# Values of two head groups in one projection, tokens stationary, and reordered query projections, in a one-core vision-tower kernel

## The chip, the core and the metric

The kernel runs on one core of a Trainium2 chip. The metric is the device time of one execution in microseconds, median of several. TensorE (PE) multiplies, VectorE (DVE), ScalarE (ACT) and GpSimd (POOL) do the element-wise work, and SyncE (SP) issues the DMAs.

## The reference

Three layers are computed one after the other for 8 batches of 256 tokens by 512 features:

```python
h = _L0_tok_ref(x, ...)                    # a long complex exponential sum: the mixer, (8, 256, 512)
h = h + attn(layernorm(h), w_q, w_k, w_v, w_o)
h = h + ffn(layernorm(h), ...)             # gated selection among 8 low-rank updates

# attn: 16 query heads, 4 key/value heads, head size 128
q = (x @ w_q).reshape(b, s, 16, 128).transpose(0, 2, 1, 3)
k = (x @ w_k).reshape(b, s, 4, 128).transpose(0, 2, 1, 3)
v = (x @ w_v).reshape(b, s, 4, 128).transpose(0, 2, 1, 3)
q, k = q * cos + rotate_half(q) * sin, k * cos + rotate_half(k) * sin
k, v = repeat(k, 4, axis=1), repeat(v, 4, axis=1)
scores = einsum('bhqd,bhkd->bhqk', q, k) / sqrt(128)
probs = softmax(scores + bias)             # causal
out = einsum('bhqk,bhkd->bhqd', probs, v)
out = out.transpose(0, 2, 1, 3).reshape(b, s, 2048) @ w_o
```

## The kernel before

**Stages.** The mixer comes first (to about 99 us of the profile), with tables built by DVE, ACT and POOL, and small matmuls in `chunk` (L1420). Its result goes through device memory (`mixed`) into the tile `x`, which holds all 8 batches. Attention follows. Its unit is a step: one batch `b` for one head group `g`, where a group is one key/value head with its four query heads. There are 4 groups of 8 batches, so 32 steps, `i = b + 8 * g`. The last layer's work is threaded into the steps of group 3 (`needs_ffn`, `needs_finish`, `needs_norm2`), and the first norm and the transposes of its tokens into those of group 0 (`needs_norm1`, `needs_xt`). Such threaded pieces are called hooks here.

**Order.** It is written out by hand: every engine has its own program, with a function `step(g, b, at)` in each, and semaphores between them. `RUNS` (L94) says which batches of a group are written out and which are a hardware loop. A step on an engine is software-pipelined: while the scores and probabilities of step i are worked on, TensorE projects keys, values and queries of step i+1 and multiplies the attention of step i-1 by `w_o`.

**Precision.** Each operand is held as a rounded high part and the rest (`w_hi`/`w_lo`, `xt_hi`/`xt_lo` and so on), and `split_product` (L1410) makes each product of three matmuls: high by high, low by high, high by low. ACT writes a high part (`split_hi`, `round_*`), and DVE or POOL the rest (`split_lo`, `*_rest`).

**A TensorE step, in order** (L1625): `scores(i)`, four heads into banks 3 to 6; `project(i+1)` (L1506), which is keys and values into the halves of bank 0, hooks, heads 0 and 1 into bank 1 (`project_q(b, 0)`), a hook with the gates' product, heads 2 and 3 into bank 2; `transpose_probs(i)` into banks 5 to 7; `out_product(i-1)` into banks 3 and 4; `transpose_v(i+1)`, two transposes of the values into bank 2; `attend(i)`, probabilities by values into banks 0 and 1. Every projection has the weight slice (128 columns) stationary and 256 tokens moving, so keys and values come out with the head dimension on the partitions. `attend` wants the values with the tokens there, and so the value half is copied to `vt` by ACT (L795), transposed, rounded into `v_hi` by ACT (`round_v`, L806), and `v_lo` is made by DVE (`v_rest`, L1138).

**ACT**: `exponents(i)`, `swap` (two half copies with the partition halves exchanged, for the rotation) of keys and of each query pair, `round_probs(i)`, `round_kq(i+1)`, `round_attn(i)`, `round_v(i+1)`. **POOL**: `normalise_probs(i)`, then `rotate(i+1)`: the sine product of keys, heads 0/1, heads 2/3 (`rotate_sin`), then their low parts (`kq_rest`). **DVE**: `masked_scores(i)` with the rest of attention i-1 in its middle, `reciprocals`, `rope` (cosine product), `rope_add`, `probs_rest(i)` (L1298), `add_output(i-1)`, `attn_rest(i, 0)`.

**Weights.** `w_qkv` of a group is four chunks of 128 by 768, `w_o` four of 128 by 512. `load_raw` (L417) loads them on SP's queue. They are split at `at == NB - 2` (the seventh step of a group) and at `at == 0`. On POOL these splits (L480) stand behind `rotate(i+1)`, and on TensorE `wait_split` stands ahead of the first projection of the next group. The first group's four splits stand on POOL between the two halves of the first norm.

Of the kernel before, what the change touches and what calls it, by code (L numbers as in the profile page):

```python
# [18 lines left out]
F32 = mybir.dt.float32  # L19
# [16 lines left out]
WC = HD + HD + QH * HD  # L36
# [65 lines left out]
def steps(engine, body):  # L102

    for g in range(NG):
        for lo, hi in RUNS[g]:
            if hi - lo == 1:
                body(g, lo, lo)
            else:
                with engine.Fori(lo, hi) as b:
                    body(g, b, lo)  # L110

# [21 lines left out]
def tower(nc, mix_c, mix_s, log_dt, log_wr, w_im, w_qkv, w_o, w_gate, w_gmul, w_upd, centers, slopes, consts, out):  # L133
    x_dram = nc.dram_tensor("mixed", [S, NB, D], F32, kind="Internal").ap()
    top = ExitStack()
    with top:
# [27 lines left out]
        fw = sb("fw", [P, KC, FC])  # L164
        dw = sb("dw", [MC, D])
        cw = sb("cw", [P, FC])
        dbs = sb("dbs", [P, KC, NE])
# [27 lines left out]
        raw_more = sb("raw_more", [P, 2, WC], F32, mixer)  # L195
        small = ExitStack()
# [62 lines left out]
        vt = sb("vt", [P, S])  # L259
# [11 lines left out]
        mt = sb("mt", [MC, S])  # L271
# [20 lines left out]
        def raw_chunk(n):  # L292
            width = WC if n % NCK < KC else D
# [15 lines left out]

        def raw_turn(n):  # L310

            return sum(raw_slot(m) == raw_slot(n) for m in range(n + 1))
# [28 lines left out]
        vt_ready, v_hi, v_lo = sem("vt_ready"), sem("v_hi_done"), sem("v_lo_done")  # L341
# [36 lines left out]

        def d_turn(bb):

            return 2 * NB - 3 - bb if isinstance(bb, int) and bb >= NB - 2 else bb
# [11 lines left out]
        def _(sp):  # L393
# [5 lines left out]
            def load_raw(n):  # L399
# [6 lines left out]
                src = w_qkv[g, k] if k < KC else w_o[g, k - KC]  # L406
                sp.dma_start(raw_chunk(n), src).then_inc(raw_in[raw_slot(n)], 16)
# [10 lines left out]
            sp.dma_start(fw[:], w_gate).then_inc(gate_in, 16)  # L418
            sp.dma_start(dw[:], w_upd).then_inc(gate_in, 16)
# [34 lines left out]
            for n in range(KC + 2, NCK * NG):  # L454
                load_raw(n)
# [15 lines left out]
        def _(pool):  # L471
            def split_lo(n):
# [3 lines left out]
                if k < KC:  # L476
                    hi, lo = wk[:, k, :], wl[:, k, :]
# [179 lines left out]
        def _(act):  # L657
            def split_hi(n):
# [3 lines left out]
                dst = wk[:, k, :] if k < KC else woh[:, k - KC, :]  # L662
# [120 lines left out]
            def swap(s, parts=range(3)):  # L783

                for j in parts:
                    view, _, _, _ = rope_view(j)
                    act.wait_ge(proj, s * 3 + (j + 1))
                    if j == 0 and (not isinstance(s, int) or s):
                        act.wait_ge(kq_rot, s * 3)
                        act.wait_ge(vt_ready, s)  # L790
                    src = banks[j][:, 0:S] if j == 0 else banks[j][:].rearrange("p (h s) -> p h s", h=2)
                    nc.scalar.activation(view(sw)[0:64], src[64:128], ACT.Copy)  # L792
                    last = nc.scalar.activation(view(sw)[64:128], src[0:64], ACT.Copy)  # L793
                    if j == 0:
                        last = nc.scalar.activation(vt[:], banks[0][:, S:2 * S], ACT.Copy)  # L795
                    last.then_inc(swapped, 1)
# [9 lines left out]
            def round_v(s, bank=2):  # L806
                act.wait_ge(vt_ready, s + 1)
                nc.scalar.activation(vh[:].rearrange("p t d -> p (t d)"), banks[bank][:, 0:S], ACT.Copy).then_inc(v_hi, 1)
# [11 lines left out]
            round_v(0, 7)  # L820
            round_kq(0, (2,))
            swap(1, (0,))
# [24 lines left out]
            def round_attn(i):  # L847
                for j in range(2):
                    act.wait_ge(pv_ready, i * 2 + (j + 1))
                    nc.scalar.activation(by_rows(oth, j), natural(banks[j]), ACT.Copy).then_inc(ot_hi, 1)  # L850

            def step(g, b, at):
                i = b + 8 * g
                exponents(i)
                swap(i + 1, (0,))
# [4 lines left out]
                swap(i + 1, (1, 2))  # L860
# [22 lines left out]
            round_probs(0)  # L883
            round_kq(1, (1,))
            swap(1, (2,))
            round_kq(1, (2,))
# [909 lines left out]
```

## Time and profile before

| | |
|---|---|
| median of three runs | 815.43 us (813.94 to 815.71) |
| profiled execution | 815.9 us, of which the recorded span is 813.8 us |
| TensorE busy | 748.4 us, 92% of the span |
| VectorE, ScalarE, GpSimd busy | 571.2, 456.3, 447.3 us |
| granted TensorE clock, mean | 0.994 of full |
| DMA | 26.47 MB, mean 33 GB/s |

The profile puts the end of a matmul by a model that includes the pipeline's latency. A matmul of 256 columns stands in it with about 280 ns, while the next one starts some 118 ns later. What a matmul costs is therefore read from the distance between starts. Times in a timeline are microseconds from the start of the span.

### The profile page before, as it was taken

Reading aid. Unit: us, or ns where it says so; the run is one execution under the profiler, and the core shown is the slowest. Engines: PE = TensorE matmul, PEld = TensorE weight load, DVE = VectorE, ACT = ScalarE, POOL = GpSimd, SP = SyncE. Lnnn points to the kernel's source line nnn. Section 1 sums busy time; section 2 is a strip of 40 time slices with the busy share of each in tenths; the row PEclk is TensorE's granted clock in tenths of the full one; section 3 lists DMA queues with packets and bytes.
Section 4 is the critical chain, followed back from the end, with each engine's and each line's share of the span. In section 5 each row is a group of like instructions: output and inputs, shape, how many; then the busy total and the mean of one; then the engine's idle time right before and its main releaser. Section 6 shows DMA issues by size and latency. Waiting matters only on the chain.

```text
span 813.8 us, 19725 instructions
## 1 busy us (share of the span) xinstructions
PE 748.4 (92%) x6968; PEld 679.0 (83%) x6968; DVE 571.2 (70%) x1603; ACT 456.3 (56%) x1252; POOL 447.3 (55%) x663
## 2 busy tenths in 40 slices
PE   0377788999999999999999999999999999999996
PEld 0166667899999999999999999999999998988873
DVE  7989868877765655565665566666655777778876
ACT  6734436565567566555575655555756645545432
POOL 1488847655545646444465654444747565565532
PEclk9999999999999999999999999999999999999999
DMA  9023741100010102000001020000100001110104
GB/s 213 0 55 86 173 130 27 39 1 0 0 41 1 53 1 79 0 0 0 0 14 40 10 69 0 0 0 0 30 24 2 1 2 27 26 26 0 27 8 96
DMA packets 32215, 26.47 MB, mean 33 GB/s; under 512 B 23134, under 2 KB 23518, under 8 KB 32166
## 3 DMA queue, kind: packets, MB, share of 16 engines
q1 hardware_dynamic: 32022, 25.77, 12.7%
q8 instruction: 28, 0.46, 0.2%
q14 instruction: 21, 0.17, 0.1%
q10 hardware_dynamic: 144, 0.07, 0.0%
HBM read 17.44 MB, written 8.39 MB: 32 GB/s over the span
## 4 chain that ended last, share of the span: by engine, by line
PE 77%; POOL 7%; DVE 7%; ACT 4%; issue 3%; DMA 1%; DVEq 0%; SPq 0%; POOLq 0%; ACTq 0%
PE bank_quad L1414 17%; PE bank_quad L1416 16%; PE bank_quad L1415 16%; PE bank_pair L1414 4%; PE bank_pair L1416 4%; PE bank_pair L1415 4%; POOL w_lo L480 2%; PE bank_quad L1426 2%; PE bank_quad L1529 2%; PE bank L1607 1%; PE bank_pair L1597 1%; PE bank L1611 1%; PE bank_pair L1607 1%; DVE bank_pair L1043 1%; POOL kq_lo L572 1%
## 5 line engine op out<-in xcount | busy, mean ns | idle before, releaser
L1414 PE MATMUL bank_quad<-xt_hi,w_hi 128*128 (+1 forms) x768 | 216.7, 282 | 1.7 <-POOL w_lo L480 0.8
L1416 PE MATMUL bank_quad<-xt_lo,w_hi 128*128 (+1 forms) x768 | 214.4, 279 | 0.0
L1415 PE MATMUL bank_quad<-xt_hi,w_lo 128*128 (+1 forms) x768 | 214.3, 279 | 0.0
L1130 DVE TENSOR_TENSOR kq<-bank_quad,cst 128x512 f32<-128x512 f32 (+1 forms) x96 | 57.8, 603 | 134.3 <-ACT swap L793 101.2
L567 POOL TENSOR_TENSOR swap<-swap,cst 128x512 f32<-128x512 f32 (+1 forms) x96 | 106.0, 1106 | 81.2 <-ACT swap L793 77.0
L1414 PEld LDWEIGHTS bank_quad<-xt_hi,w_hi 128*128 128x128 f32 x768 | 144.2, 188 | 3.4 <-POOL w_lo L480 1.5
L1416 PEld LDWEIGHTS bank_quad<-xt_lo,w_hi 128*128 128x128 f32 x768 | 144.2, 188 | 0.0
L1415 PEld LDWEIGHTS bank_quad<-xt_hi,w_lo 128*128 128x128 f32 x768 | 143.9, 187 | 0.0
L387 POOL TENSOR_TENSOR spare<-cst 1x1 f32<-1x1 f32 x86 | 17.8, 208 | 200.3 <-DVE rinv L1296 139.7
L838 ACT ACTIVATE sm<-sm,mx 128x128 f32<-128x128 f32 (+1 forms) x256 | 113.6, 445 | 20.6 <-DVE mx L1284 20.6
L792 ACT ACTIVATE swap<-bank_quad 64x512 f32<-64x512 f32 (+1 forms) x96 | 50.3, 524 | 118.0 <-PE bank_quad L1416 115.1
L605 POOL TENSOR_SCALAR sm<-sm,rinv 128x128 f32<-128x128 f32 (+1 forms) x256 | 104.4, 421 | 0.9
L850 ACT ACTIVATE ot_hi<-bank_quad 128x512 fp32r<-128x512 f32 x64 | 37.8, 597 | 110.2 <-PE bank_quad L1416 110.2
L1136 DVE TENSOR_TENSOR kq<-kq,swap 128x512 f32<-128x512 f32 (+1 forms) x96 | 94.9, 1012 | 4.7 <-POOL swap L567 4.7
L572 POOL TENSOR_TENSOR kq_lo<-kq,kq_hi 128x256 fp32r<-128x256 f32 x93 | 78.5, 869 | 19.9 <-ACT kq_hi L804 19.9
L1275 DVE TENSOR_TENSOR ot_lo<-bank_quad,ot_hi 128x512 fp32r<-128x512 f32 x64 | 43.4, 677 | 25.7 <-ACT ot_hi L850 25.6
L1414 PE MATMUL bank_quad<-wo_hi,ot_hi 128*128 128x512 f32 x132 | 54.5, 413 | 0.4 <-DVE ot_lo L1275 0.4
L1416 PE MATMUL bank_quad<-wo_lo,ot_hi 128*128 128x512 f32 x132 | 51.9, 394 | 0.0
L1415 PE MATMUL bank_quad<-wo_hi,ot_lo 128*128 128x512 f32 x132 | 51.8, 393 | 0.0
L793 ACT ACTIVATE swap<-bank_quad 64x512 f32<-64x512 f32 (+1 forms) x96 | 49.9, 520 | 1.1
L1416 PE MATMUL bank_pair<-wo_lo,ot_hi 128*128 128x512 f32 x124 | 48.4, 390 | 0.0
L1415 PE MATMUL bank_pair<-wo_hi,ot_lo 128*128 128x512 f32 x124 | 48.2, 389 | 0.0
(332 smaller groups left out, 1867.7 us busy)
## 6 DMA issues: line engine op xcount, KB each, us to landing
mixed<-st SPq DMA_DIRECT2D x32, 128.0 KB, 2.0
x<-mixed SPq DMA_DIRECT2D x32, 128.0 KB, 3.1
out<-x SPq DMA_DIRECT2D x32, 128.0 KB, 2.3
raw<-in_w_qkv SPq DMA_DIRECT2D x8, 384.0 KB, 3.7
raw<-in_w_o SPq DMA_DIRECT2D x10, 256.0 KB, 2.7
norm_mem<-in_w_qkv SPq DMA_DIRECT2D x6, 384.0 KB, 3.7
norm_mem<-in_w_o SPq DMA_DIRECT2D x6, 256.0 KB, 2.8
cim<-in_mix_s SPq DMA_DIRECT2D x4, 256.0 KB, 7.9
```

The source lines that it names most:

```text
L567: nc.gpsimd.tensor_tensor(view(sw), view(sw), table(sinT), ALU.mult).then_inc(rot_sin, 1)
L572: nc.gpsimd.tensor_tensor(flat(kl), part(kq), flat(kh).bitcast(F32), ALU.subtract).then_inc(kq_lo, 1)
L605: last = nc.gpsimd.tensor_scalar(sm[:, j, cols], sm[:, j, cols], rinv[:, 2 * j + t:2 * j + t + 1], 1.0, ALU.mult, ALU.mult)
L792: nc.scalar.activation(view(sw)[0:64], src[64:128], ACT.Copy)
L793: last = nc.scalar.activation(view(sw)[64:128], src[0:64], ACT.Copy)
L838: last = nc.scalar.activation(sm[:, j, cols], sm[:, j, cols], ACT.Exp, scale=-1.0, bias=mx[:, n:n + 1], accum_out=rsum[:, n:n + 1])
L1130: v.tensor_tensor(view(kq), src, table(cosT), ALU.mult).then_inc(kq_cos, 1)
L1136: v.tensor_tensor(view(kq), view(kq), view(sw), ALU.add).then_inc(kq_rot, 1)
L1275: v.tensor_tensor(by_rows(otl, j), natural(banks[j]), by_rows(oth, j).bitcast(F32), ALU.subtract).then_inc(ot_lo, 1)
L1414: mmul(dst, lh, rh, start=start and k == 0, stop=False, skip_group_check=True)
L1415: mmul(dst, ll, rh, start=False, stop=False, skip_group_check=True)
L1416: last = mmul(dst, lh, rl, start=False, stop=stop and k == n - 1, skip_group_check=True)
```

## The change

Head groups are paired. In the even group of a pair (0 and 2) the values of both groups are projected by one `project_v`, with the tokens stationary and 2 x 128 weight columns moving, so that they come out in the orientation that `attend` wants. The pair's other values go from bank 0 into `v_next` (ACT), to device memory (`later_v`), and come back a batch at a time in the odd group. `transpose_v` and the copy to `vt` are gone. `w_hi`/`w_lo` and the raw chunks are 128 columns wider, so the even groups' chunks have 896 columns (split by ACT, POOL and DVE in full), the odd groups' 768. Keys go to bank 7 in even groups and to bank 0 in odd ones, and attention's result to banks 1 and 2 instead of 0 and 1. The hooks now all stand between the two query pairs, and heads 2 and 3 and the values follow them. TensorE's steps of groups 0 and 2 are written out, since the order differs at their start. The feed-forward weights `fw`, `dw` and the tile `mt` move into the raw weight buffer and are loaded in group 3.

TensorE:

```diff
+            def project_v(g, b):
+                pair = lambda w, k: w[:, k, HD:].rearrange("p (n c) -> p n c", c=HD)[:, 0:6:5, :]
+                for t in range(TT):
+                    rows = slice(t * P, (t + 1) * P)
+                    last = split_product(banks[0][:, t * 2 * HD:(t + 1) * 2 * HD].rearrange("p (n c) -> p n c", c=HD),
+                                         [(xt_h[:, b, k, rows], xt_l[:, b, k, rows], pair(wk, k), pair(wl, k))
+                                          for k in range(KC)])
+                last.then_inc(v_ready, 1)
+
+            def project(s, g, b, between):
+                if g % 2:
+                    pe.wait_ge(v_next_done, (g // 2 + 1) * NB)
+                project_k(g, b)
                 pe.wait_ge(ot_lo, s * 2 - 3)
-                project_kv(b)
-                after_kv()
+                project_q(g, b, 0)
+                between()
                 pe.wait_ge(ot_lo, s * 2 - 2)
-                project_q(b, 0)
-                pe.wait_ge(v_lo, s)
-                before_last()
-                project_q(b, 1)
+                project_q(g, b, 1)
+                if g % 2 == 0:
+                    pe.wait_ge(v_lo, s)
+                    pe.wait_ge(v_next_done, b + (g // 2) * NB)
+                    project_v(g, b)
...
                 pe.wait_ge(pt_lo, i * 3)
+                pe.wait_ge(swapped, i * 3 + 4)
+                pe.wait_ge(kq_cos, i * 3 + 4)
...
                 out_product(i - 1)
-                transpose_v(i + 1)
```

In `between()` the order is: token transposes of the first norm, those of the second (`transpose_tokens(b + 6)`), `update_product(b - 3)`, and then the gates' product, which waits for `xt_hi`. DVE, ACT and SP:

```diff
                 reciprocals(i)
-                rope(i + 1, 0)
+                rope(i + 1, 0, key_bank(*step_after(g, b, at)))
+                rope(i + 1, 1)
+                rope_add(i + 1, 0)
                 if needs_finish(g, at):
                     finish(b - 3)
                 if needs_xt(g, at):
                     xt_rest(b + 2)
-                rope(i + 1, 1)
-                rope_add(i + 1, 0)
                 if needs_ffn(g, at):
                     gate_read(b - 2)
                     gate_scores(b - 2)
+                rope_add(i + 1, 1)
                 rope(i + 1, 2)
-                rope_add(i + 1, 1)
                 rope_add(i + 1, 2)
...
                 exponents(i)
-                swap(i + 1, (0,))
+                swap(i + 1, (0,), key_bank(*after))
+                swap(i + 1, (1,))
                 if needs_xt(g, at):
                     xt1(b + 2)
                 if needs_ffn(g, at):
                     xt2(b - 2, 3)
-                swap(i + 1, (1, 2))
+                swap(i + 1, (2,))
...
+                keep_next_v(*after)
                 round_attn(i)
-                round_v(i + 1)
+                round_v(*after)
...
+            def load_v(g, b):
+                sp.wait_ge(v_stored, 16 * (g // 2 + 1) * NB)
+                if b:
+                    sp.wait_ge(v_lo, g * NB + b)
+                sp.dma_start(later, v_dram[b]).then_inc(v_loaded, 16)
```

The opening changes likewise: keys, heads 0/1, tokens of batch 1, heads 2/3, values of batch 0, keys of batch 1, scores of step 0, then heads 0/1, tokens of batch 2, heads 2/3 and values of batch 1, and `transpose_probs(0)`.

## Rows read from the trace of the kernel before

**Rows 1.** The page: busy time, share of the span and instructions of each engine
```profile
PE 748.4 (92%) x6968; PEld 679.0 (83%) x6968; DVE 571.2 (70%) x1603; ACT 456.3 (56%) x1252; POOL 447.3 (55%) x663
```
**Rows 2.** Busy time of each engine in single steps of groups 0, 2, 3, and the end
```profile
201.70:222.50 20.80, 20.80 (x152) 19.49 (x151) 16.11 (x46) 12.38 (x34) 10.38 (x19) 1.00 0.00 0
423.30:444.00 20.70, 20.38 (x143) 18.71 (x142) 13.08 (x37) 11.90 (x33) 14.67 (x19) 1.00 0.16 51
463.90:483.80 19.90, 19.90 (x143) 18.60 (x142) 11.96 (x36) 13.37 (x36) 14.48 (x20) 1.00 0.26 81
716.00:740.60 24.60, 24.60 (x173) 22.23 (x172) 19.51 (x67) 12.80 (x36) 14.49 (x24) 1.00 0.09 21
765.20:813.80 48.60, 40.83 (x213) 29.74 (x211) 35.82 (x115) 15.60 (x40) 16.59 (x28) 0.97 0.19 44
```
**Rows 3.** TensorE's timeline, one step of group 2: start, duration, line, operation
```profile
403.38 0.38 PE L1519 MATMUL bank_quad<-cst,vt 128*128 128x128 f32 x2
...
404.41 0.27 PE L1415 MATMUL bank_quad<-pt_hi,v_lo 128*128 128x256 f32 x1
404.52 0.28 PE L1416 MATMUL bank_quad<-pt_lo,v_hi 128*128 128x256 f32 x1
...
405.69 0.39 PE L1597 MATMUL bank_quad<-kq 128*128 128x128 f32 x2
...
408.00 0.28 PE L1414 MATMUL bank_quad<-xt_hi,w_hi 128*128 128x256 f32 x1
...
416.48 0.60 PE L1607 MATMUL bank_pair<-cst,sm 128*128 128x128 f32 x4
...
423.29 0.38 PE L1519 MATMUL bank_quad<-cst,vt 128*128 128x128 f32 x2
```
**Rows 4.** The same step on POOL and DVE: probabilities, and the chain ahead of `attend`
```profile
412.04 1.63 POOL L605 TENSOR_SCALAR sm<-sm,rinv 128x128 f32<-128x128 f32 x4
417.91 0.69 DVE L1130 TENSOR_TENSOR kq<-bank_quad,cst 128x512 f32<-128x512 f32 x1 [1.21 <-ACT swap L793]
420.93 1.27 DVE L1301 TENSOR_TENSOR pt_lo<-bank,pt_hi 128x512 fp32r<-128x512 f32 x2
```
**Rows 5.** The page's DMA issues: size, median us from issue to landing
```profile
x<-mixed SPq DMA_DIRECT2D x32, 128.0 KB, 3.1
```
**Rows 6.** The change to group 2: a weight split on POOL, and TensorE's wait
```profile
426.70 1.86 POOL L480 TENSOR_TENSOR w_lo<-norm_mem,w_hi 128x768 fp32r<-128x768 f32 x1
428.62 0.39 PE L1414 MATMUL bank_quad<-xt_hi,w_hi 128*128 128x256 f32 x1 [0.28 <-POOL w_lo L480]
```
**Rows 7.** The opening on POOL: weight splits, and the second half of the norm
```profile
101.81 3.79 POOL L480 TENSOR_TENSOR w_lo<-raw_more,w_hi 128x768 fp32r<-128x768 f32 x2
106.13 0.18 POOL L387 TENSOR_TENSOR spare<-cst 1x1 f32<-1x1 f32 x1 [0.53 <-DVE norm L1164]
```
**Rows 8.** TensorE's waits for `pt_lo` in the first two steps
```profile
136.94 0.47 PE L1414 MATMUL bank_quad<-pt_hi,v_hi 128*128 128x512 f32 x1 [1.84 <-DVE pt_lo L1301]
160.24 0.47 PE L1414 MATMUL bank_quad<-pt_hi,v_hi 128*128 128x512 f32 x1 [0.79 <-DVE pt_lo L1301]
```
**Rows 9.** A step of group 3: its start, and what the gates wait for, on four engines
```profile
743.17 0.39 PE L1597 MATMUL bank_quad<-kq 128*128 128x128 f32 x2
748.30 1.12 PE L1547 MATMUL bank_pair<-dw,mt 72*128 72x512 f32 x2
748.44 0.98 DVE L1112 TENSOR_SCALAR norm_mem<-x,norm 128x512 f32 x2
749.48 0.38 ACT L792 ACTIVATE swap<-bank_quad 64x256 f32<-64x256 f32 x1
750.12 0.60 PE L1490 MATMUL bank_quad<-cst,norm_mem 128*128 128x128 f32 x4
750.76 0.60 ACT L780 ACTIVATE norm_mem<-bank_quad 128x512 f32<-128x512 f32 x1
753.21 0.73 POOL L567 TENSOR_TENSOR swap<-swap,cst 128x256 f32<-128x256 f32 x1
```

More of the change, by code:

```diff
@@ L99, with steps @@
 ]
-def steps(engine, body):
+def steps(engine, body, unrolled=()):
     for g in range(NG):
-        for lo, hi in RUNS[g]:
+        for lo, hi in [(b, b + 1) for b in range(RUNS[g][0][0], NB)] if g in unrolled else RUNS[g]:
             if hi - lo == 1:
@@ L110, in steps, with w_width, key_bank, step_after @@
                     body(g, b, lo)
+def w_width(g):
+    return WC if g % 2 == 0 else WC - HD
+def key_bank(g, b):
+    return 7 if g % 2 == 0 or (isinstance(b, int) and b == 0) else 0
+def step_after(g, b, at):
+    return (g, b + 1) if at < NB - 1 else (g + 1, 0)
 def needs_xt(g, at):
@@ L308, in wait_split, with raw_parts @@
                 engine.wait_ge(w_lo_dve, by_dve)
+        def raw_parts(n):
+            return 2 if n % NCK < KC and n // NCK % 2 == 0 else 1
         def raw_turn(n):
-            return sum(raw_slot(m) == raw_slot(n) for m in range(n + 1))
+            return sum(raw_parts(m) for m in range(n + 1) if raw_slot(m) == raw_slot(n))
         cst_in, par_in, mix_in, gate_in = sem("cst_in"), sem("par_in"), sem("mix_in"), sem("gate_in")
@@ L781, in xt2, with swap @@
                                          banks[first_bank + q][:], ACT.Copy).then_inc(xt_hi, 1)
-            def swap(s, parts=range(3)):
+            def swap(s, parts=range(3), keys=7):
                 for j in parts:
@@ L789, in swap @@
                         act.wait_ge(kq_rot, s * 3)
-                        act.wait_ge(vt_ready, s)
-                    src = banks[j][:, 0:S] if j == 0 else banks[j][:].rearrange("p (h s) -> p h s", h=2)
+                    src = banks[keys][:, 0:S] if j == 0 else banks[j][:].rearrange("p (h s) -> p h s", h=2)
                     nc.scalar.activation(view(sw)[0:64], src[64:128], ACT.Copy)
[L793 to L796, printed above, removed]
+                    nc.scalar.activation(view(sw)[64:128], src[0:64], ACT.Copy).then_inc(swapped, 1)
             def round_kq(s, parts=range(3)):
@@ L819, in _ @@
             split_hi(KC + 1)
-            round_v(0, 7)
             round_kq(0, (2,))
+            round_v(0, 0)
+            keep_next_v(0, 0)
             swap(1, (0,))
@@ L883, in _ @@
             round_probs(0)
+            swap(1, (2,))
             round_kq(1, (1,))
-            swap(1, (2,))
             round_kq(1, (2,))
+            keep_next_v(0, 1)
             round_attn(0)
-            round_v(1)
+            round_v(0, 1)
             for k in range(KC + 2, NCK):
@@ L896, in _ @@
             round_probs(last)
-            round_attn(last)
+            round_attn(last, 0)
             def scale_normed(bb):
@@ L1289, in masked_scores @@
                         attn_rest(i - 1, 1)
-                if with_v:
-                    v_rest(i)
+                if v_group is not None:
+                    v_rest(v_group, i)
             def reciprocals(i, halves=range(2)):
@@ L1365, in _ @@
             reciprocals(last, (1,))
-            v_rest(last)
+            v_rest(NG - 1, last)
             add_output(last - 1, NB - 2, (0,), 0)
@@ L1711, in _ @@
             pe.wait_ge(x_added, 2 * last)
-            attend(last)
+            attend(last, 0)
             pe.wait_ge(ot_lo, 2 * last + 1)
```

212 lines of the change are left out of this document (133 added, 79 removed).

## The prediction

> **What bounds the kernel now.** I read the page first: TensorE is busy for 748.4 of 813.8 us, the next engine for 571.2 [rows 1]. Shares average over stages, so the second view is the busy time in single steps. A step without hooks takes 19.9 us and TensorE works through all of it, while DVE has 12.0, ACT 13.4 and POOL 14.5 even in the step with weight splits. A step of group 0 with token transposes takes 20.8, one of group 3 24.6, TensorE full in both; DVE is at 19.5 there, which makes group 3 the stage to watch [rows 2]. Third, the timeline of one step shows what fills it. From one value transpose to the next are 423.29 - 403.38 = 19.91 us: scores 405.69 to 408.00 (2.31), 72 projection matmuls until 416.48 (8.48, so 0.118 each), 12 transposes and 24 output matmuls until 423.29 (6.81), two value transposes and `attend` 2.3 [rows 3]. So in some 28 of 32 steps TensorE's own work sets the time. It waits only at a group's start (0.8: 20.7 against 19.9) [rows 2, 6], in the opening [rows 8], and at the end, where it is busy for 40.8 of 48.6 us and DVE for 35.8 [rows 2].
>
> **Value transposes: gone.** The price of one comes from the steps with and without eight token transposes, which have the same form: (20.8 - 19.9) / 8 = 0.11 us [rows 2]. There are 32 pairs, so 64 x 0.11 = **-7.0 us**. What a removed matmul gives back is worth its full price only where TensorE stays the bound, which the parts below check.
>
> **Projection of values: same work, moved.** Before, 32 steps have 12 value matmuls of 256 columns; after, 16 steps have 24 of 2 x 128. That is 384 both times, at 0.118 in sum 45 us, so **0** at the same pace. The pace with a jump of 640 columns in the moving operand is in no row. The nearest is `attend`'s second part, whose two runs of 128 are apart in its destination: 404.52 - 404.41 = 0.11 [rows 3], which would make -3 us. The other end is a product in full fp32, at 0.11 for 128 columns, so 0.22 for 256, and +39 us. I take 0.118, since an operand with one jump is nearest to the same form without it; 0.11 stays in the range and 0.22 is a rival.
>
> On a jump there is a rule. The row shows two runs of 128 columns at full pace [rows 3]. The Trainium skill (PSUM — Partial Sum Buffer, Specifications) says that any non-contiguous access pattern slows matmuls significantly; by the row the sum stays at -5.3, by the rule taken at its word it would end on the slow side. The row disagrees for runs this long, though only in the destination.
>
> **Even steps get longer, odd ones shorter**: 19.9 - 0.22 + 1.41 = 21.1 and 19.9 - 0.22 - 1.41 = 18.3. In even steps the other engines have 1.2 us more. In odd ones every chain loses 1.4 to 1.6 us of room, so each must be looked at.
> - Probabilities: POOL ends them at 413.67, and TensorE wants them at 416.48 [rows 3, 4], 2.8 us of room. The transposes come 1.41 earlier: 1.4 left.
> - Rotation of heads 2/3, then `probs_rest`, then `attend`: anchored at the end of the projection, it ends at 422.20, and `attend` follows at 423.51 [rows 3, 4]. Without value transposes 1.1 us are left. `rope_add` of heads 0/1 now stands ahead of it, where it is hidden by the wait for heads 2/3 (1.21 us) [rows 4].
> - Keys first, without a wait for attention's result, and the query waits later: no loss. `keep_next_v` and `round_v` cost ACT at most what `vt` and `round_v` did.
> - The way through device memory: a value tile is asked for when `v_rest` of the step has run, and the batch's load takes about as long as one of the mixer's, 3.1 us [rows 5], while `round_v` comes some 10 us later. Queued behind `load_v` on SP's queue are the weights, which have nearly a step of room. I cost it at nothing; if that cover went, the attention of an odd step would wait for a DMA.
> So group 1 should be TensorE's alone.
>
> **Starts of groups: less gain, +1.5 us.** TensorE waits for the low parts of the next weights, which POOL makes after `kq_rest`; that chain is anchored at `transpose_probs`. From there TensorE reaches the next group 0.22 sooner, so the saving isn't had in these three steps: +0.6. Group 2's chunks are 896 wide. POOL has three in a row, each 1.86 us for 768 [rows 6], so 0.31 more: +0.9. ACT's and DVE's splits grow beside it. Bounds: 0 and 3 us.
>
> **Opening, -1.9 us.** Between the two halves of the first norm POOL makes the low parts of four chunks. Each grows by 0.3, 1.2 in all, of which 0.53 us of idle time takes a part [rows 7]; the norm's second half starts the chain to the first projection: +0.7. Behind it TensorE waited 1.84 and 0.79 us for `pt_lo` [rows 8]. Now the first values (1.41 more per batch) lie ahead of these waits and the probabilities' chain, which hangs on the scores, isn't longer. The 2.6 us of idle time is filled by work that the sum above had counted in full: -2.6. Bounds: 0 and -4. The wider loads at the very start stand ahead of the mixer's inputs, which are wanted much later: 0.
>
> **Group 3, +1.9 us.** Its steps lose 1.63 like other odd ones, to 23.0, but the hooks are in another order. With the step's start at 743.17 as zero: scores and keys to 3.7, heads 0/1 to 6.55, the normed tokens (ready at 748.44 + 0.98, so 6.25) transposed to 7.4, `update_product` 1.8 (748.30 to 750.12) to 9.25, then the gates, which want ACT's copies. ACT ends its exponents at 6.3 (749.48) and has ahead of these copies the keys' swap (0.8) and, as new, that of heads 0/1 (1.2, which waits for 6.55); with 0.6 and 0.5 for the copies they are there at 9.6 [rows 9]. A wait of 0.4 in each of four steps, some 0.3 in the one where the gates begin: **+1.9**. Bounds: 0 and +1.6 in each of five steps. The loop across engines is the danger: DVE's `rope_add` of the keys waits for POOL, which is done with probabilities and its first product at 10.8 (753.21 + 0.73), and it now stands ahead of `finish` and the gates' reads. Masks, exponents, probabilities, `rope_add`, `finish`, gates, rotation, `probs_rest`, gates, outputs, statistics and masks again make 22.8 us by DVE's, ACT's and POOL's durations, 0.6 under TensorE's 23.4.
>
> **End, +0.2 us.** It is DVE's chain, which the change doesn't touch. DVE's lag behind TensorE stays, so the last step's 0.22 isn't had.
>
> **Sum**: -7.0 + 0 + 1.5 - 1.9 + 1.9 + 0.2 = -5.3. The profiled execution's 815.9 becomes 810.6. It lies 0.5 above the median of 815.43, and by that the forecast is **810.1**.
>
> **The rivals.**
> - *Value matmuls at the pace of `attend`, and no wait for the gates*: -5.3 - 3.1 - 1.9, so 805 to 807. For it: the measured 0.11 [rows 3]. Against it: all projections run at 0.118.
> - *Group 3 stays at 24.6*: its loop, not TensorE, sets the step. Five steps lose 1.2 more than forecast: 816. For it: DVE has 19.5 us of work for 23.4, in order [rows 2]. Against it: my count leaves 0.6.
> - *It doesn't do what it says*: the transposes' time was shared with something else that ends no earlier, and nothing moves: 815. Against it: TensorE has no gap in a step [rows 2, 3].
> - *Odd steps stay at 19.9 everywhere*, held by ACT, DVE and POOL in a ring or by the values' way back, while even ones pay 21.1: some 14 steps without 1.6 us, 824 to 829. For it: only 1.1 us are left ahead of `attend`.
> - **Slower: the jump in the moving operand.** If a matmul of 2 x 128 columns takes longer than 0.118 + 5.3 / 384 = 0.132 us, the change loses. At 0.22 it is 849, and the even steps show it alone, at 23.6 instead of 21.1. For it: no row has that form. Against it: the row with the jump in the destination.
>
> **How the numbers follow.** Forecast 0.54, with its own range 808 to 812.5; the faster pace 0.12; group 3 at 24.6 0.12; no effect 0.06; odd steps held 0.09; slow jump 0.07. From no effect a measurement of this kernel tells 0.2%, 1.6 us. Faster: 0.54 + 0.12 = 0.66. Same: 0.12 + 0.06 = 0.18. Slower: 0.16. The range that leaves out the last two and the fringe of the first goes from 806 to 816.5.
>
> **What would show it.** Steps of group 2 at 21.1 and of group 1 at 18.3, value matmuls 0.118 apart; waits of 1.0 us for `w_lo` at groups 1 and 3 and 1.9 at group 2; the waits for `pt_lo` of the first two steps gone or under a microsecond; group 3 at 23.4 with a wait for `xt_hi`'s copy ahead of the gates. A wait for `pt_lo` or for POOL's probabilities in group 1, a group 3 above 24, or value matmuls apart by more than 0.13 would make it wrong.

## The result and the profile after

The changed kernel takes **827.28 us** (median of five runs, 826.18 to 828.13), against 815.43 (813.94 to 816.29) for the kernel before beside it: 1.0144 times the time, 95% interval 1.0129 to 1.0159. The forecast was 810.1 with a range from 806 to 816.5, so both the size and the sign were wrong. The profiled execution took 828.13 us with a span of 826.1, which is 12.3 more than before's 813.8.

The page after, busy time of each engine, and the row of the granted clock in 40 slices:

```profile
PE 742.3 (90%) x6904; PEld 673.2 (81%) x6904; DVE 584.1 (71%) x1603; ACT 444.9 (54%) x1236; POOL 438.9 (53%) x663
...
PEclk9999999899999999999999999999999999999999
```

Against [rows 1] TensorE does 64 matmuls fewer and is busy 6.1 us less, so the work did go. DVE's busy time rose by 12.9 us with the same number of instructions, 1603. Their durations in sum rose by 7.4 us (658.0 to 665.5), of it 3.6 in the additions of the rotation, so part of the rise is instructions that took longer; the other part, less overlap of one with the next, was not followed up. And one slice, at 145 to 165 us, has a lower clock.

The length of each step (from the first matmul of `scores(i)` to that of the next, in TensorE's timeline) tells where the time went. "Forecast" is the sum of the prediction's terms for that stretch:

| stretch | before | after | change | forecast |
|---|---|---|---|---|
| start to the end of step 0 | 139.3 | 140.7 | +1.4 | +1.2 |
| steps 1 to 5 (the token hooks) | 106.3 | 126.3 | **+20.0** | +5.2 |
| step 6 and group 1 up to step 13 | 160.1 | 148.8 | -11.3 | -10.0 |
| steps 14 to 22 | 180.2 | 187.8 | +7.6 | +9.0 |
| steps 23 to 25 | 60.4 | 54.8 | -5.6 | -4.7 |
| steps 26 to 30 (the last layer's hooks) | 121.5 | 121.2 | **-0.3** | -6.3 |
| from the start of step 31 | 46.1 | 46.5 | +0.4 | +0.2 |
| sum | 813.8 | 826.1 | +12.3 | -5.4 |

Two rows miss: +14.8 us in group 0 and +6.0 in group 3. The rest is 3.2 better than forecast. The first row is the least sure: with the same code in front of them, the first projection starts anywhere from 109.66 to 111.08 us in the traces of the changed kernel and of those made from it below. The windows of single steps, of groups 0, 1, 2 and 3, show the same (start and end, length, busy time and instructions of PE, PEld, DVE, ACT and POOL, granted clock, DMA share, GB/s), to be read beside [rows 2]:

```profile
194.60:219.10 24.50, 22.07 (x163) 20.68 (x162) 17.50 (x46) 12.15 (x34) 10.08 (x19) 1.00 0.02 6
306.30:324.60 18.30, 18.30 (x131) 17.07 (x130) 11.87 (x36) 12.19 (x34) 10.14 (x17) 1.00 0.03 8
498.60:519.60 21.00, 21.00 (x154) 19.77 (x153) 12.30 (x37) 11.06 (x32) 8.90 (x16) 1.00 0.02 8
730.30:754.90 24.60, 23.61 (x159) 20.58 (x159) 20.72 (x68) 12.35 (x36) 14.48 (x25) 1.00 0.02 5
```

Groups 1 and 2 are TensorE's alone, at 18.3 and 21.0. In group 0 and group 3 TensorE, full in every such step of before [rows 2], now has gaps of 2.4 and 1.0 us.

**What TensorE waits for in group 3.** Its waits from 657 to 782 us, a stretch in which before has none (engine, tile and line, what it waited for: us in total, times, longest; "issue" is a wait for which the profile shows no releaser):

```profile
PE bank_quad L1695 <- DVE x L1289: 2.3, 4, 0.6
PE bank_quad L1627 <- ACT norm_mem L859: 1.6, 4, 0.5
PE bank_quad L1627 <- issue: 1.6, 1, 1.6
```

The first stands ahead of `scores(i)`, for DVE's addition of the output of an earlier step: DVE is late at the end of its step. The other two stand ahead of the gates' product, in steps 27 to 30 and in step 26.

**What TensorE waits for in group 0.** Its waits from 122 to 257 us, those of 0.5 and more:

```profile
PE bank_pair L1705 <- DVE xt_lo L1216: 11.2, 4, 3.9
PE bank_quad L1509 <- DVE kq L1224: 1.9, 1, 1.9
PE bank_pair L1695 <- POOL kq_lo L651: 0.5, 1, 0.5
```

L1705 is the first transpose of `transpose_probs(i)`. It stands behind a wait for `xt_lo`, the low part of a later batch's tokens, which DVE makes in `xt_rest` (L1216): the transposed tokens lie in banks 5 and 6 until `xt_rest` has read them, and the transposes of the probabilities write to the same banks. Here is step 3 on TensorE, on DVE and on POOL, in three timelines (start, duration, line, operation, and in brackets the idle time before and what ended it):

```profile
207.45 0.28 PE L1511 MATMUL bank_quad<-w_lo,xt_hi 128*128 128x256 f32 x1
210.16 0.52 PE L1705 MATMUL bank_pair<-cst,sm 128*128 128x128 f32 x3 [2.44 <-DVE xt_lo L1216]
```

```profile
202.55 0.69 DVE L1224 TENSOR_TENSOR kq<-bank_quad,cst 128x512 f32<-128x512 f32 x1 [1.52 <-ACT swap L871]
205.98 2.72 DVE L1230 TENSOR_TENSOR kq<-kq,swap 128x256 f32<-128x256 f32 x1 [2.74 <-POOL swap L646]
208.63 0.68 DVE L1216 TENSOR_TENSOR xt_lo<-bank_pair,xt_hi 128x512 f32 x1
209.23 0.68 DVE L1216 TENSOR_TENSOR xt_lo<-bank,xt_hi 128x512 f32 x1
```

```profile
203.98 1.27 POOL L684 TENSOR_SCALAR sm<-sm,rinv 128x256 f32<-128x256 f32 x3
205.23 3.19 POOL L646 TENSOR_TENSOR swap<-swap,cst 128x256 f32<-128x256 f32 x3
```

TensorE's last projection starts at 207.45; the transposes start at 210.16, when `xt_lo` is there. DVE was idle from 203.24 to 205.98, waiting for the sine product of the keys, which POOL makes only behind the probabilities. Then `rope_add` of the keys took 2.72 us. Only behind it comes `xt_rest`. In before's order `xt_rest` stood **ahead** of this pair of wait and slow addition; the diff moves it behind.

### The profile page after: what moved, and what is told of

It reads as the page before. It is cut to its first block, busy times and chain, and to the rows that moved or that the text cites. A ratio compares the mean times of both kernels' runs of the same rounds, so it can differ in the third digit from the quotient of the medians.

```text
span 826.1 us, 19513 instructions
## 1 busy us (share of the span) xinstructions
PE 742.3 (90%) x6904; PEld 673.2 (81%) x6904; DVE 584.1 (71%) x1603; ACT 444.9 (54%) x1236; POOL 438.9 (53%) x663
## 4 chain that ended last, share of the span: by engine, by line
PE 61%; DVE 12%; POOL 12%; issue 9%; ACT 3%; DVEq 0%; DMA 0%; POOLq 0%; ACTq 0%
PE bank_quad L1509 13%; PE bank_quad L1510 13%; PE bank_quad L1511 13%; PE bank_pair L1509 3%; PE bank_pair L1510 3%; PE bank_pair L1511 3%; POOL sm L684 3%; POOL w_lo L559 2%; PE bank_pair L1705 1%; PE bank L1705 1%; PE bank L1709 1%; POOL kq_lo L651 1%; DVE bank_pair L1137 1%; PE bank L1509 1%; PE bank_pair L1695 1%
## 5 line engine op out<-in xcount | busy, mean ns | idle before, releaser
L1509 PE MATMUL bank_quad<-xt_hi,w_hi 128*128 128x256 f32 (+1 forms) x568 | 159.6, 281 | 0.0
L1510 PE MATMUL bank_quad<-xt_hi,w_lo 128*128 128x256 f32 (+1 forms) x568 | 158.9, 280 | 0.0
L1511 PE MATMUL bank_quad<-xt_lo,w_hi 128*128 128x256 f32 (+1 forms) x568 | 158.6, 279 | 0.0
L1509 PEld LDWEIGHTS bank_quad<-xt_hi,w_hi 128*128 128x128 f32 x568 | 106.8, 188 | 0.0
L1510 PEld LDWEIGHTS bank_quad<-xt_hi,w_lo 128*128 128x128 f32 x568 | 106.6, 188 | 0.0
L1511 PEld LDWEIGHTS bank_quad<-xt_lo,w_hi 128*128 128x128 f32 x568 | 106.3, 187 | 0.0
L651 POOL TENSOR_TENSOR kq_lo<-kq,kq_hi 128x256 fp32r<-128x256 f32 x93 | 69.7, 776 | 59.4 <-ACT kq_hi L879 59.4
L870 ACT ACTIVATE swap<-bank_quad 64x512 f32<-64x512 f32 (+1 forms) x78 | 43.4, 556 | 85.3 <-PE bank_quad L1511 84.5
L1224 DVE TENSOR_TENSOR kq<-bank_quad,cst 128x512 f32<-128x512 f32 (+1 forms) x78 | 50.0, 641 | 52.2 <-ACT swap L871 51.9
L1509 PE MATMUL bank_pair<-wo_hi,ot_hi 128*128 128x512 f32 x124 | 48.2, 389 | 0.0
```

Source lines behind the costliest of these rows:

```text
L651: nc.gpsimd.tensor_tensor(flat(kl), part(kq), flat(kh).bitcast(F32), ALU.subtract).then_inc(kq_lo, 1)
L1224: v.tensor_tensor(view(kq), src, table(cosT), ALU.mult).then_inc(kq_cos, 1)
L1509: mmul(dst, lh, rh, start=start and k == 0, stop=False, skip_group_check=True)
L1510: mmul(dst, ll, rh, start=False, stop=False, skip_group_check=True)
L1511: last = mmul(dst, lh, rl, start=False, stop=stop and k == n - 1, skip_group_check=True)
```

## The experiments

The theory of the first four: the order of DVE's step alone makes the loss of group 0, and a like order that of group 3. Rival theories: the values ahead of the hooks' end (more TensorE work before the wait), the memory round trip, or the operand with a jump. In each ratio the kernel before ran beside on the same chip, and 815.35 to 815.78 us were its medians. Where two kernels are compared that ran on different chips, these medians say how far that can be trusted: to some 0.4 us.

### The tokens' low parts first

```diff
                 rope(i + 1, 1)
+                if needs_xt(g, at):
+                    xt_rest(b + 2)
                 rope_add(i + 1, 0)
                 if needs_finish(g, at):
                     finish(b - 3)
-                if needs_xt(g, at):
-                    xt_rest(b + 2)
```

> The changed kernel with one move on DVE: in a step of group 0 the low parts of the next tokens (xt_rest) stand ahead of rope_add of the keys instead of behind it. Theory A (order): TensorE stands ahead of transpose_probs for xt_lo because xt_rest waits behind a rope_add that itself waits for POOL's probabilities and sine products. Then the waits of 4.0, 2.6, 2.6 and 2.6 us go, and with them the low clock that followed the first and the last; steps 1 to 5 fall from 29.4, 24.5, 24.5, 26.1, 21.9 to about 22 each, and the kernel to 827.3 - 16 = 811 to 813 us. Rival B (load): group 0's even steps give DVE, ACT or POOL more work than a step holds, whatever its order. Then the waits move to another semaphore and the kernel stays above 823 us.

Measured: 812.82 us, 0.9967 times the kernel before (0.9957 to 0.9977). Steps 1 to 5 took 22.75, 21.86, 21.86, 21.86, 21.86: from 126.3 down to 110.2 us. No wait for `xt_lo` is left in the same window. Two lines moved on one engine give 14.5 us back and turn a loss of 1.4% into a gain of 0.3%. `rope_add` of the keys still takes 2.7 us in steps 1 to 4 of this kernel; nobody waits for what is behind it. Everything else of the change was in this kernel too, so neither the jump, nor the round trip, nor the place of the values makes the loss by itself.

### The end of the last layer first

```diff
                 rope(i + 1, 1)
-                rope_add(i + 1, 0)
                 if needs_finish(g, at):
                     finish(b - 3)
                 if needs_xt(g, at):
                     xt_rest(b + 2)
+                rope_add(i + 1, 0)
```

This is the second of two kernels. In the first, `rope_add` of the keys stands between `finish` and `xt_rest`, so that only group 3 is changed.

> The changed kernel with one move on DVE: in a step of group 3 finish stands ahead of rope_add of the keys. Theory A: in group 3 DVE goes round in 24.6 us because it idles for POOL's sine product with finish and the gates' reads queued behind, and group 3 gets back most of the 1.2 us a step that it missed: steps 27 to 30 at 23.4 to 23.8, kernel at 822 to 824 us. Rival B: DVE's own work and the gates' chain set 24.6, and the kernel stays within 1.5 us of 827.3.

> Both moves together. Theory A: the gains add up, 807 to 810 us, the forecast's sum. Rival B: 820 us or more.

Measured: 823.47 us (1.0103, 1.0086 to 1.0119) and 808.38 us (0.9913, 0.9897 to 0.993). Steps 27 to 30 went from 24.3 to 24.7 us to 23.4 to 23.5 in both. So `finish` behind the keys' addition cost 3.8 us in the one (827.28 - 823.47) and 4.4 in the other (812.82 - 808.38), in steps 26 to 30 4.4 us in both, and it is independent of group 0. TensorE's wait for DVE ahead of `scores` is gone. What is left are its waits ahead of the gates, in the second kernel, from 640 to 782 us:

```profile
PE bank_quad L1627 <- issue: 1.6, 1, 1.6
PE bank_quad L1627 <- ACT norm_mem L859: 1.1, 4, 0.3
```

The single one of 1.6 us is in step 26, the first with gates. That step takes 23.01 us here as in the changed kernel, and 23.00 in the kernel before.

### The new order in the kernel before

```diff
@@ the kernel before @@
-                if needs_xt(g, at):
-                    xt_rest(b + 2)
                 rope(i + 1, 1)
                 rope_add(i + 1, 0)
+                if needs_xt(g, at):
+                    xt_rest(b + 2)
```

> The kernel before with only the disputed order put in: xt_rest behind rope of heads 0/1 and rope_add of the keys, in all steps of group 0 that have tokens. Nothing else of the change. Theory A: the order alone makes TensorE wait ahead of transpose_probs, longer than in the changed kernel since no value projection lies ahead: three to four steps lose 3 to 5 us each, 828 to 835 us. Rival B: without the wider steps the order is harmless, within 2 us of 815.4.

Measured: 832.38 us, 1.0207 times (1.0189 to 1.0224). Steps 1 to 5 became 29.7, 25.08, 23.38, 24.83, 22.31, 19.0 us more in sum; no other step changed by more than 0.4. TensorE's waits from 138 to 250 us:

```profile
PE bank_pair L1607 <- DVE xt_lo L1122: 7.2, 3, 2.4
PE bank_pair L1607 <- issue: 4.6, 1, 4.6
```

(The second stands ahead of the transposes of step 1, as the others do in steps 2 to 4; the profile shows no releaser for it.) The order is sufficient by itself: without anything else of the change it costs 17 us.

### Is part of it the clock?

The waits for `xt_lo` in the changed kernel are 11.2 us, yet 14.5 came back. The granted clock, the last figure but two, in the gap of step 1 and behind it, then in the gap of step 4 and behind it:

```profile
154.00:158.00 4.00, 0.58 (x6) 0.39 (x4) 3.70 (x3) 0.00 (x0) 2.71 (x3) 0.92 0.00 0
158.00:162.00 4.00, 3.55 (x15) 3.39 (x16) 3.56 (x7) 1.92 (x4) 0.00 (x0) 0.50 0.00 0
232.50:235.00 2.50, 0.35 (x3) 0.38 (x4) 2.50 (x5) 0.00 (x0) 0.41 (x1) 1.00 0.00 0
236.00:238.00 2.00, 2.00 (x7) 1.61 (x6) 2.00 (x4) 2.00 (x6) 0.70 (x2) 0.50 0.00 0
```

Behind both gaps TensorE runs at half clock, 1.2 instead of 2.4 GHz. To price this, matmuls without use fill the gap ahead of the wait, six of 512 columns in full fp32 in one kernel and three in the other:

```diff
                 if needs_xt(g, at):
+                    pe.wait_ge(s_masked, i * 4 + 4)
+                    keep_warm(6, 3)
                     pe.wait_ge(xt_lo, b * 2 + 6)
                 transpose_probs(i)
```

> The changed kernel with six unneeded matmuls (fp32, 512 columns, into bank 3, free by then) ahead of TensorE's wait for xt_lo in the token steps of group 0; they take at most 2.7 us, about the length of the wait that they stand in front of. Nothing is computed differently. Theory A: besides the waits themselves (4.0 and three of 2.6 us), the idle time costs the clock in one or two steps (granted clock 0.5 for some 5 us behind the wait of 4.0 us, and again in step 4); with the gap filled the clock stays at 1.0, steps 1 and 4 lose 2.5 and 1.6 us, and the kernel comes to 823 to 824 us while the waits for xt_lo stay. Rival: the low clock comes from elsewhere or costs nothing on the path: 826 to 829 us.

Measured: 839.57 us, 1.0295 times (1.0277 to 1.0312), far off what was expected, because the filler was sized wrong. TensorE in step 2 of that kernel:

```profile
181.77 5.32 PE L1535 MATMUL bank_quad<-cst 128*128 128x512 f32 x12
186.92 0.60 PE L1705 MATMUL bank_pair<-cst,sm 128*128 128x128 f32 x4
```

The six take 186.92 - 181.77 = 5.15 us, 0.86 each (two records of 0.43), not the 0.45 or less that I had counted with, and overrun the gap by 2.6. Step 1 was still 1.7 us shorter than in the changed kernel. The run is of no use for the total; hence three matmuls:

> As e5, with three unneeded matmuls instead of six: one of them took 0.86 us in e5, so three fill 2.6 us, the length of the shorter waits. e5 said that the filler's length, not the clock, then sets the step (21.9 + 5.2 = 27.1 us in steps 2 to 5), and that step 1 is 1.7 us shorter than in the changed kernel all the same. Theory A: steps 2 and 3 stay at 24.5, step 4 falls from 26.1 to 24.5, step 1 from 29.4 to 26.7, while step 5, which had no wait, grows to 24.5; without that one the kernel would be at 823, with it at 825 to 826 us. Rival: steps 1 and 4 stay where they are, kernel at 829 to 831 us.

Measured: 827.22 us, 1.0137 times (1.012 to 1.0154). Windows of it over the same places:

```profile
150.00:160.00 10.00, 8.86 (x62) 7.07 (x61) 5.70 (x7) 3.39 (x7) 7.39 (x14) 1.00 0.00 0
160.00:170.00 10.00, 10.00 (x60) 8.78 (x59) 7.42 (x19) 4.49 (x13) 2.31 (x3) 1.00 0.04 15
232.00:242.00 10.00, 10.00 (x55) 8.32 (x54) 7.68 (x12) 3.70 (x9) 2.31 (x3) 1.00 0.05 15
```

Full clock throughout. Step 1 fell from 29.41 to 26.56 and step 4 from 26.08 to 24.51, as expected: the low clock costs 2.85 + 1.57 = 4.4 us. The gap of step 1 is as long as without filler: from the first of the three matmuls (155.18) to the transposes (159.06) are 3.9 us. So the 2.85 us come from behind it. Step 5 rose from 21.86 to 24.5 by the filler itself: it has no gap to fill, and its three matmuls take 2.6 us. The steps together are 1.8 us shorter, the span 0.9 (825.2 against 826.1), the median the same; the total is 1 to 2 us above what was expected. Of that, 0.8 lies ahead of step 1, where step 0 ends at 141.44 instead of 140.68 and nothing was changed; the rest stays open.

The trace of the kernel with `finish` alone moved shows the same thing without a filler. It has the gap of 2.6 us in steps 2 to 4 as well, and here the half clock follows that of step 3 and not that of step 4:

```profile
211.00:214.00 3.00, 3.00 (x9) 2.32 (x8) 3.00 (x6) 1.90 (x6) 1.90 (x3) 0.50 0.08 26
235.00:238.00 3.00, 2.41 (x17) 2.27 (x18) 2.90 (x6) 1.75 (x4) 0.00 (x0) 1.00 0.00 0
```

Step 3 takes 26.12 us there and step 4 24.52, where the changed kernel has 24.49 and 26.08: again 1.6 for the low clock. The clock is a part of the loss, but it is no cause of its own: where the gaps are gone or short, as with `xt_rest` first and in the next section, no low clock follows the transposes of steps 1 to 5. (With `xt_rest` first it is low once, from 139.4 to 142.8 us, behind the opening's wait of 1.9.)

### Why does the addition take 2.72 us?

Beside it POOL runs its next two sine products, the last ending at 208.42, and `rope_add` ends just behind. In groups 1 and 3, where one product follows, the same shape takes 1.5 us. A kernel in which POOL waits with them until DVE is done tells an addition that POOL's products hold up from one that is slow by itself:

```diff
             def rotate(s, apart=False):
...
+                    if apart and j == 1:
+                        pool.wait_ge(kq_rot, s * 3 + 1)
...
-                rotate(i + 1)
+                rotate(i + 1, needs_xt(g, at))
```

> The changed kernel, where in the token steps of group 0 POOL holds back its sine product of heads 0/1 until DVE's rope_add of the keys is done. Theory C: that rope_add lasts 2.7 us instead of 0.4 because DVE and POOL can't both run such an operation, and POOL's next two sine products are issued back to back in front of it. Then rope_add falls to under 0.8 us, xt_rest comes 2 us sooner, TensorE's waits fall from 4.0 and 2.6 to 2.0 and 0.6 us, the clock stays up, and the kernel comes to 815 to 819 us with the order of the change untouched. Rival: rope_add is long for another reason; it stays above 2 us and the kernel stays at 826 us or more, since POOL has only been delayed.

Measured: 815.18 us, 0.9989 times (0.998 to 0.9999). Step 3 on DVE, then on POOL:

```profile
199.95 0.42 DVE L1232 TENSOR_TENSOR kq<-kq,swap 128x256 f32<-128x256 f32 x1 [2.74 <-POOL swap L646]
200.31 0.69 DVE L1218 TENSOR_TENSOR xt_lo<-bank_pair,xt_hi 128x512 f32 x1
...
201.85 1.75 DVE L1232 TENSOR_TENSOR kq<-kq,swap 128x512 f32<-128x512 f32 x1 [0.26 <-POOL swap L646]
```

```profile
199.19 0.72 POOL L646 TENSOR_TENSOR swap<-swap,cst 128x256 f32<-128x256 f32 x1
200.53 2.52 POOL L646 TENSOR_TENSOR swap<-swap,cst 128x512 f32<-128x512 f32 x2 [0.62 <-DVE kq L1232]
```

2.72 us became 0.42 for the same instruction, and 12.1 of the 14.5 us came back, with `xt_rest` still behind it (the two kernels ran on different chips; by the steps it is 13.1 of 16.1). Steps 1 to 5 took 24.41, 22.5, 22.23, 22.23 and 21.86, without low clock. So the order alone, with an addition that isn't held, costs 3.0 us in these steps; the rest of the loss needs both, the order and the held addition.

The Trainium skill (SBUF — State Buffer, Who interferes with whom) says that a DVE instruction with two inputs in SBUF contends with a GpSimd instruction that reads SBUF; of the port pair that the two engines share it says that it is an exclusive lock and that issue order decides who blocks. The trace agrees: both inputs of `rope_add` are in SBUF, POOL's product starts first (205.91 against 205.98 in step 3 of the changed kernel), and `xt_rest`, with one input in PSUM, takes at most 0.69 us in every trace, also beside POOL's work. That DVE gets no turn between two products of POOL is the trace's alone.

### TensorE alone in group 3, and the opening

The first of two kernels takes the second one above (`finish` and `xt_rest` first), puts group 3's copies for the gates ahead of the swap of heads 0 and 1 on ACT, and also moves `finish` ahead of their cosine product on DVE. The second adds the opening: on ACT `swap(1, (2,))` ahead of `round_probs(0)`, on DVE `rope(1, 2)` ahead of `probs_rest(0)`.

```diff
@@ ACT, step @@
                 swap(i + 1, (0,), key_bank(*after))
-                swap(i + 1, (1,))
                 if needs_xt(g, at):
+                    swap(i + 1, (1,))
                     xt1(b + 2)
                 if needs_ffn(g, at):
                     xt2(b - 2, 3)
+                if not needs_xt(g, at):
+                    swap(i + 1, (1,))
                 swap(i + 1, (2,))
@@ DVE, step @@
-                rope(i + 1, 1)
                 if needs_finish(g, at):
                     finish(b - 3)
+                rope(i + 1, 1)
@@ ACT, the opening (second kernel) @@
-            round_probs(0)
             swap(1, (2,))
+            round_probs(0)
@@ DVE, the opening (second kernel) @@
-            probs_rest(0)
             rope(1, 2)
+            probs_rest(0)
```

> As e3 (both moves), and in group 3 ACT copies the normed tokens ahead of the swap of heads 0/1 instead of behind it, with finish also ahead of rope of heads 0/1 on DVE. Theory A: the wait of 0.4 to 0.6 us ahead of the gates goes, so steps 27 to 30 fall from 23.45 to about 23.0 each: 806 to 807 us, 1.6 to 2 us under e3. Rival: the ring through DVE and POOL sets 23.45 by itself, and nothing changes (within 0.5 us of e3's 808.4).

> As e6, and in the opening the swap of heads 2/3 of batch 1 stands ahead of round_probs(0) on ACT, and their rope ahead of probs_rest(0) on DVE. In the changed kernel the first attend waits 1.9 us for that rope, since its result now goes to the bank that holds these queries. Theory A: the wait becomes one for pt_lo and is 1.0 us shorter, so e6 less 1 us (805 to 806). Rival: the batch's rest (xt_rest, rope_add) is late in any case, and nothing changes within 0.4 us.

Measured: 805.2 us (0.9872, 0.9855 to 0.9888) and **803.97 us** (803.15 to 804.45; 0.9852, 0.9836 to 0.9869). In the first, steps 27 to 30 are TensorE's alone:

```profile
687.90:710.90 23.00, 23.00 (x161) 20.81 (x160) 19.78 (x68) 12.32 (x36) 14.12 (x25) 1.00 0.02 6
```

Steps 27 to 30 are at 22.94 to 22.95, where the kernel before has 24.5 to 24.7. The two moves together were worth 3.2 us (808.38 - 805.2, on different chips), more than the 1.6 to 2 expected: four times 0.5 in these steps, and 0.8 in step 26, where 0.8 of its wait of 1.6 is left. Which of the two moves gives it was not separated. The opening gives 1.2 more. In the changed kernel the first `attend` waits not for `pt_lo`, as in [rows 8], but for a cosine product, and in the last kernel for `pt_lo` again, 0.85 us shorter:

```profile
138.50 0.47 PE L1509 MATMUL bank_quad<-pt_hi,v_hi 128*128 128x512 f32 x1 [1.92 <-DVE kq L1224]
```

```profile
138.31 0.47 PE L1511 MATMUL bank_quad<-pt_hi,v_hi 128*128 128x512 f32 x1 [1.07 <-DVE pt_lo L1397]
```

So the last kernel is 1.5% faster than the one before, where the change as it was made costs 1.4%; the new orders of copies and opening, and `finish` ahead of the cosine product, were not tried in the kernel before, and how much of the 1.5% they would give there is open.

## Why the prediction was wrong, and where it was right

**Value transposes, -7.0: right.** Where TensorE sets the time, the forecast lengths of 18.3 and 21.1 stand at 18.26 and 20.99. A pair of steps (one with values, one without) went from 39.82 to 39.25.

**Projection of values, 0 at 0.118: right, and slightly pessimistic.** The 24 value matmuls of a step of group 2 start 0.114 apart (508.00 to 510.74), so a step with values is 0.1 shorter than forecast. That is 1.6 us in 16 steps. The slow jump (0.22, or the break-even of 0.132) did not occur. The price of that rival was itself misread: the experiments show 0.86 us for 512 columns in full fp32, so 0.43 for 256 as an estimate from it, where the prediction has 0.22. Such a matmul stands in two records, and the prediction's 0.11 for 128 columns is the price of one. The Trainium skill's rule (PSUM — Partial Sum Buffer, Specifications) that non-contiguous patterns slow matmuls significantly stands there as a property of PSUM. The value matmuls don't test it, since their jump is in the moving operand, in SBUF, and they write to PSUM without one; `attend`'s second part does, with two runs of 128 in its destination, and at 0.11 [rows 3] the rule isn't borne out for runs of that length.

**Odd steps hold: right.** Group 1 has no wait in a step, neither for probabilities nor for `pt_lo` nor for the loads of `later_v` (on the page 2.0 us from issue to landing, where 3.1 had been taken).

**Starts of groups, +1.5: wrong for two of three.** In the kernel before, the two steps around each start are 0.8 us longer than their neighbours. After, those at group 2 are 1.5 longer (18.68 and 22.13 against 18.26 and 21.0), so 0.7 more, where 1.1 was forecast; the wait for `w_lo` is 0.8, not the 1.9 forecast. At groups 1 and 3 nothing is waited for: the steps are 21.0 and 18.26 like the others, which gives 0.8 back at each. In sum that is -0.9 where +1.5 was forecast. I had anchored POOL's chain at `transpose_probs`. But heads 2 and 3 now come before the values: in step 6 POOL's last `kq_lo` ends 16.85 us behind the step's start, against 16.73 before, while the step ends 0.9 us later. The low parts of the weights follow at once and have that time. This gain the working missed.

**Opening, -1.9: partly.** Both waits for `pt_lo` are gone. The first projection comes at 110.15 instead of 109.71, 0.4 later where 0.7 was forecast, but with a scatter of 1.4 us between traces this can't tell the two. The first wait was replaced by one of 1.9 for the cosine product of heads 2 and 3, which the change had moved back. I counted idle time as filled without asking what is late next.

**Group 0, the failed step: +14.8 us of the 17.7 that the span missed.** The prediction put the new order of DVE's step in group 0 at nothing, without a reason, and no rival names it. Its general argument, that TensorE has no gap in a step and other engines have room, was made from busy time [rows 2], and the new order of DVE was checked only for group 3. The prediction says of `rope_add` of the keys that "it now stands ahead of `finish` and the gates' reads"; it stands ahead of `xt_rest` as well, and TensorE waits for that in the middle of its step. Part of the price was in before's trace, from which I took no such row. There DVE's addition waits for POOL and takes 2.75 us in step 1:

```profile
153.09 2.75 DVE L1136 TENSOR_TENSOR kq<-kq,swap 128x256 f32<-128x256 f32 x1 [1.53 <-POOL swap L567]
```

```profile
152.34 3.21 POOL L567 TENSOR_TENSOR swap<-swap,cst 128x256 f32<-128x256 f32 x3
```

In steps 2 to 4 of before it takes 1.49, since POOL's third product waits for ACT's swap of heads 2 and 3 and only one follows at once. Here step 2 on DVE and on POOL:

```profile
173.85 1.49 DVE L1136 TENSOR_TENSOR kq<-kq,swap 128x256 f32<-128x256 f32 x1 [0.48 <-POOL swap L567]
```

```profile
173.09 1.97 POOL L567 TENSOR_TENSOR swap<-swap,cst 128x256 f32<-128x256 f32 x2
175.55 1.29 POOL L567 TENSOR_TENSOR swap<-swap,cst 128x512 f32<-128x512 f32 x1 [0.49 <-ACT swap L793]
```

The change has both query pairs' swaps earlier against POOL's products, so all three run back to back in steps 1 to 4, and the 1.49 becomes 2.72. In before nobody waits for what is behind the addition, so it costs nothing there. From such rows the sum can be made, here with those of step 3 after: ahead of the addition `xt_rest` would run from 203.24 to 204.5, 3.0 us before TensorE wants it at 207.56; the wait of 2.74 and the addition of 2.72 put ahead of it make it 2.4 late, which is the gap. With before's 1.49 in place of 2.72 the same sum gives 1.2 late, an estimate: the rows of before would have shown a loss in each of these steps, but half of it.

What makes up the +14.8: four gaps, 4.0 and three of 2.6 us (from 0.11 behind the start of the last value matmul to the transposes), together 11.8, and the low clock behind the first and the last, 4.4. That is 16.2, and putting `xt_rest` first took 16.1 out of these five steps (126.3 to 110.2). Against it, those 110.2 are 1.3 under the 111.5 forecast, 0.5 of it by the faster value matmuls; the rest I did not separate.

**Group 3, +1.9 forecast for its hooks: +7.9 measured.** Its steps stay at 24.6, which was a rival, with a chance of 0.12. Three parts can be told apart. The wait ahead of the gates in steps 27 to 30 was right: with `finish` first, the steps are at 23.44 to 23.5, where 23.4 was forecast, and with the copies and `finish` moved further at 22.95, so it is 0.5. In step 26, where the gates begin, the wait was mis-sized: 1.6 us where some 0.3 was forecast, so 1.3 of this stage's 6.0, which `finish` first doesn't give back. What failed in the other steps is the ring, counted at 22.8: it takes 24.6, and TensorE waits for DVE at its end. The cost is in the order, since moving `finish` alone ahead of the addition and its wait brings 23.45. Here DVE's timeline in step 30 of the changed kernel:

```profile
765.92 1.48 DVE L1230 TENSOR_TENSOR kq<-kq,swap 128x256 f32<-128x256 f32 x1 [1.75 <-POOL swap L646]
767.33 0.74 DVE L1363 SCALAR_TENSOR_TENSOR x<-bank_pair,norm,x 128x512 f32 x1
```

DVE is idle for 1.75 us with `finish` behind it. The additions are held by POOL as well, 1.48 instead of 0.42 for the keys and 1.72 instead of 0.68 for heads 0 and 1. With `finish` first the keys' addition still takes 1.48 and the other 0.69. The count of 22.8 doesn't give the durations that it is made of, so which of them was short isn't shown, nor how the 1.2 us a step divide between the idle time and the held additions.

**End, +0.2:** +0.4.

Of the rivals, the one that gives 824 to 829 ("odd steps stay at 19.9 everywhere") held the time by chance: its mechanism did not happen, as group 1 at 18.26 shows. The right rival was missing.

## What to carry to other kernels

When a change reorders a helper's instructions, list for **every** stage that shares this code what now stands behind each wait, and who waits for that. An engine busy for 16 of 21 us has room only if nothing that another engine needs is queued behind its waits. Take the duration of a moved instruction from the stage where it will run: one that nobody waits for can be held for 2 us in the trace without showing in the time, and that becomes due as soon as something is put behind it. And ask what will run beside it after the change: the same addition took 1.49 in three steps of before and 2.72 in the same steps after.

## What the runs showed of the hardware

- `rope_add` of 128x256 fp32, both inputs in SBUF, takes 0.42 us with POOL idle and 2.72 with two of POOL's sine products back to back beside it. It isn't held for one POOL instruction but ends only behind both (step 3 after): POOL 205.23 + 3.19 = 208.42, DVE 205.98 + 2.72 = 208.70. Behind one such product it takes 1.48. For 128x512 it is 0.68 and 1.75.
- In the changed kernel the clock was halved behind a gap of 4.0 us and behind one of 2.6, but not behind two others of 2.6 us in steps 2 and 3, which have the same work around them. With `finish` moved it was the gap of step 3 and not that of step 4. What tells these apart stays open. Half clock stretched TensorE's work by 2.85 and 1.57 us.
- A 512-column matmul of full fp32 takes 0.86 us, in two records of 0.43.
- Value matmuls with the tokens stationary and two runs of 128 moving columns, 640 apart, start 0.114 us apart, against 0.118 for 256 columns without a jump and weights stationary.
